# A share for every edge: one lookup list walked by POOL alone, or split between POOL's gathers and one-hot products on chip

## The reference

```
def _L2_gnn_ref(feature, src, dst, W_s, W_t, W_attn, W_fc, b_fc):
    z = proj_s[src] + proj_t[dst]
    z = jnp.where(z >= 0, z, NEG_SLOPE * z)
    e = (z @ W_attn.T)[:, 0]
    m = jax.ops.segment_max(e, src, num_segments=n)
    e_exp = jnp.exp(e - m[src])
    denom = jax.ops.segment_sum(e_exp, src, num_segments=n)
    alpha = e_exp / denom[src]
    msg = feature[src] * alpha[:, None]
    agg = jax.ops.segment_sum(msg, dst, num_segments=n)
```

## Time and profile before

| | us |
|---|---|
| median of 3 runs (9783.69 to 9792.57) | 9786.06 |
| the profiled execution, its own time | 9778.72 |
| its span in the trace | 9777.0 |
| POOL's first instruction of `share_in` | at 6859.21 |
| end of the last gather of `share_in` | at 7421.35 |
| PE's first instruction of the next phase | at 7428.20 |

### The profile page before, as it was taken

One profiled execution on the slowest core, in us unless ns is written; L12 is line 12 of the kernel. 1 busy time (PEld: TensorE's weight loads), 2 busy tenths in 40 slices (PEclk: granted clock), 3 DMA queues, 4 the chain that ended last, 5 costly groups with the idle time before them and its releaser, 6 DMA issues. The chain is left out here.

```text
span 9777.0 us, 155051 instructions
## 1 busy us (share of the span) xinstructions
PE 6076.9 (62%) x21338; PEld 3661.3 (37%) x21339; DVE 5653.9 (58%) x19482; ACT 3099.9 (32%) x10799; POOL 4876.5 (50%) x5997
## 2 busy tenths in 40 slices
PE   4666877756768887677999945444003678500277
PEld 3554233324543433455666611111002557400165
DVE  4666988873558776354445455555001458755664
ACT  2665022211554443254444400000000466411046
POOL 1333177756632212664444467775666652455252
PEclk8998577777989998799999966666556999755599
DMA  2332000004876654596666632332002797411057
GB/s 84 134 132 96 0 1 1 1 1 151 284 256 215 214 206 173 181 302 233 236 234 234 222 98 90 91 90 66 1 0 76 234 302 217 144 42 42 23 178 229
DMA packets 779248, 1347.62 MB, mean 138 GB/s; under 512 B 139839, under 2 KB 546391, under 8 KB 779156
## 3 DMA queue, kind: packets, MB, share of 16 engines
q1 hardware_dynamic: 208564, 650.10, 19.0%
q10 hardware_dynamic: 413792, 410.91, 13.2%
q0 software_dynamic: 156800, 285.65, 10.5%
HBM read 751.95 MB, written 594.32 MB: 138 GB/s over the span
## 5 line engine op out<-in xcount | busy, mean ns | idle before, releaser
L1435 PE MATMUL node_p_out<-w,node_h_t 128*128 128x512 f32 (+3 forms) x7840 | 2614.7, 466 | 379.1 <-ACT node_h_t L1463 141.9
L990 PE MATMUL merge_banks<-merge_rows,merge_mask 128*128 x6264 | 1680.7, 425 | 744.0 <-SPq L959 464.5
L1435 PEld LDWEIGHTS node_p_out<-w,node_h_t 128*128 128x128 f32 x7840 | 1357.1, 197 | 1077.7 <-issue 734.9
L990 PEld LDWEIGHTS merge_banks<-merge_rows,merge_mask 128*128 128x128 f32 x6264 | 1278.1, 211 | 1146.6 <-issue 954.0
L972 DVE TENSOR_SCALAR merge_mask<-ramp,dst_at,soft_at_step 128x128 f32<-128x128 f32 x2349 | 847.2, 366 | 1069.8 <-PE merge_banks L990 950.3
L1078 POOL DMA_INDIRECT merge_rows<-h,merge_take_i x1176 | 1125.1, 957 | 655.6 <-issue 249.4
L1022 ACT COPY merge_total<-merge_banks 128x256 f32<-128x256 f32 x1568 | 577.6, 369 | 1251.5 <-PE merge_banks L990 1135.4
L1613 PE MATMUL score_table<-score_at_high,score_at_low 128*128 128x392 f32 x784 | 565.6, 827 | 588.8 <-DVE score_at_high L1574 584.0
L1009 ACT COPY merge_banks<-merge_held 128x256 f32<-128x256 f32 x1568 | 588.1, 376 | 897.5 <-DMA merge_held<-own 643.3
L1353 POOL TENSOR_TENSOR node_inv_std<-node_var,node_minus_half 128x4 f32<-128x4 f32 x392 | 437.0, 1115 | 751.0 <-DVE node_var L1311 750.0
L1463 ACT ACTIVATE node_h_t<-node_p_turn 128x256 f32<-128x256 f32 x1568 | 594.7, 385 | 349.6 <-PE node_p_turn L1413 344.9
(11 more groups left out here) (409 smaller groups left out, 9678.3 us busy)
## 6 DMA issues: line engine op xcount, KB each, us to landing
h<-node_out SPq DMA_DIRECT2D x196, 512.0 KB, 5.7
merge_held<-own ACTq DMA_DIRECT2D x196, 512.0 KB, 5.8
x<-merge_total ACTq DMA_DIRECT2D x196, 512.0 KB
node_x<-x SPq DMA_DIRECT2D x196, 512.0 KB, 5.9
node_x<-in_x SPq DMA_DIRECT2D x194, 512.0 KB
h<-node_rows_h SPq DMA_DIRECT2D x98, 512.0 KB, 2.7
merge_held<-h ACTq DMA_DIRECT2D x98, 512.0 KB
mix<-merge_total ACTq DMA_DIRECT2D x98, 512.0 KB
```

What stands on the lines that cost most here:

```text
L990: nc.tensor.matmul(banks[:, bass.ds(nc.s_assert_within(at[2 * j + 1], 0, (BANKS - 1) * 512, skip_runtime_bounds_check_because=small), D)], ...
L1435: ins = nc.tensor.matmul(p_out[w][g % banks][:, 0:n], h_t[g][:, c * P:(c + 1) * P], matrix[:, c, :], start=c == 0, stop=c == 1)
```

## The change

Of the 49 groups of eight tiles, the first `GATHERED` = 25 (200 tiles) are still gathered by POOL, and the last `TURNED` = 24 (192 tiles) are looked up on chip by the other engines, in the same phase.

- In `src_out`, PE transposes the four blocks of `share` into PSUM, and DVE copies them to `table`, which is the tile `by_place`. The four DMAs to `shares` stay.
- In `share_in`, POOL copies eight columns of places at once, issues eight gathers, and itself copies a group's eight results into `out` (`keep`). The copy of group i-1 stands behind the gathers of group i. POOL waits for its own copies. DVE has no part in it any more.
- DVE splits all places into `high` and `low` with four chained instructions. For each of its 192 tiles it makes `at_low` and `at_high` (`hots`), and three tiles later it picks (`pick`): the `tensor_tensor_reduce` over 392 columns of `at_high` and the product in PSUM. Each eight tiles it copies the picked columns to `out`.
- PE transposes `at_low` of tile t (`turn`), then multiplies the table by `low_t` of tile t-1 (`look_up`), f32 with 392 columns.
- ACT copies the transposed `at_low` from PSUM to the f32 `low_t`.
- These four streams share rings of RING = 4 buffers, with waits on each other's counts.

```
-def shares_by_edge(nc, k, shares, out):
+def shares_by_edge(nc, k, shares, table, out):
...
+    NI, HALF, RING = k.NT // U, U // 2, 4
+    TURNED = NI // 2
+    GATHERED = NI - TURNED
+    START = GATHERED * U
...
+            def gathers(i, half, uses):
+                nc.gpsimd.tensor_copy(take_i[:, half, :], columns(k.pos_i, i * U, U)).then_inc(indexed, 1)
+                pool.wait_ge(indexed, i + 1)
+                pool.sem_inc(turn_pool, 1)
                 for j in range(U):
...
+                    nc.gpsimd.indirect_dma_start(got[:, half, j:j + 1], None, shares,
+                                                 bass.IndirectOffsetOnAxis(take_i[:, half, j:j + 1], 0)).then_inc(got_in[half], 16)
+
+            def keep(i, half, uses):
+                pool.wait_ge(got_in[half], 16 * U * uses)
+                pool.sem_inc(turn_pool, 1)
+                nc.gpsimd.tensor_copy(columns(out, i * U, U), got[:, half, :]).then_inc(copied, 1)
+                pool.wait_ge(copied, i + 1)
+                pool.sem_inc(turn_pool, 1)
+
+            gathers(0, 0, 1)
+            gathers(1, 1, 1)
+            keep(0, 0, 1)
+            with pool.Fori(1, GATHERED // 2) as i:
+                gathers(2 * i, 0, i + 1)
+                keep(2 * i - 1, 1, i)
+                gathers(2 * i + 1, 1, i + 1)
+                keep(2 * i, 0, i + 1)
+            if GATHERED % 2:
+                gathers(GATHERED - 1, 0, GATHERED // 2 + 1)
+            keep(2 * (GATHERED // 2) - 1, 1, GATHERED // 2)
+            if GATHERED % 2:
+                keep(GATHERED - 1, 0, GATHERED // 2 + 1)
...
+            chain = Chain(dve, digits)
+            chain(nc.vector.tensor_scalar(part_i[:], k.pos_i[:], 7, None, ALU.logical_shift_right))
+            chain(nc.vector.tensor_copy(high[:], part_i[:]))
+            chain(nc.vector.tensor_scalar(part_i[:], k.pos_i[:], P - 1, None, ALU.bitwise_and))
+            chain(nc.vector.tensor_copy(low[:], part_i[:]))
+
+            def hots(t, j):
+                later(dve, turned, t - RING + 1)
+                nc.vector.tensor_scalar(at_low[j % RING][:], k.ramp[:, 0:P], columns(low, t + START), None, ALU.is_equal
+                                        ).then_inc(low_hot, 1)
+                later(dve, picked_n, t - RING + 1)
+                nc.vector.tensor_scalar(at_high[j % RING][:], k.ramp[:, 0:k.NT], columns(high, t + START), None, ALU.is_equal
+                                        ).then_inc(high_hot, 1)
+
+            def pick(t, j):
+                dve.wait_ge(rowed, t + 1)
+                dve.wait_ge(high_hot, t + 1)
+                later(dve, picked_n, t)
+                nc.vector.tensor_tensor_reduce(junk[:], at_high[j % RING][:], p_row[j % RING][:, 0:k.NT], 1.0, 0.0,
+                                               ALU.mult, ALU.add, picked[:, j:j + 1]).then_inc(picked_n, 1)
+                if j == U - 1:
+                    dve.wait_ge(picked_n, t + 1)
+                    nc.vector.tensor_copy(columns(out, t + START - U + 1, U), picked[:]).then_inc(kept, 1)
+                    dve.wait_ge(kept, t // U + 1 if isinstance(t, int) else (t >> 3) + 1)
+
+            walk(dve, [(0, hots), (3, pick)])
...
+            def turn(t, j):
+                pe.wait_ge(low_hot, t + 1)
+                later(pe, low_copied, t - 1)
+                nc.tensor.transpose(p_turn[j % 2][:, 0:P], at_low[j % RING][:], k.ident_bf[:]).then_inc(turned, 1)
+
+            def look_up(t, j):
+                pe.wait_ge(low_copied, t + 1)
+                later(pe, picked_n, t - RING + 1)
+                nc.tensor.matmul(p_row[j % RING][:, 0:k.NT], low_t[j % RING][:], table[:, 0:k.NT], start=True, stop=True
+                                 ).then_inc(rowed, 1)
+
+            walk(pe, [(0, turn), (1, look_up)])
...
+                act.wait_ge(turned, t + 1)
+                later(act, rowed, t - RING + 1)
+                nc.scalar.copy(low_t[j % RING][:], p_turn[j % 2][:, 0:P]).then_inc(low_copied, 1)
...
-def shares_by_source(nc, k, cols, shares):
+def shares_by_source(nc, k, cols, shares, table):
...
+            dve.wait_ge(turned, 1)
+            nc.vector.tensor_copy(table[:], p[:]).then_inc(s_done, 1)
+
+        @block.tensor
+        def _(pe):
+            pe.wait_ge(step, 2)
+            for b in range(B):
+                ins = nc.tensor.transpose(p[:, b * P:(b + 1) * P], share[:, b, :], k.ident[:])
+            ins.then_inc(turned, 1)
```

More of the change, by code:

```diff
@@ L1100, in merge, with walk, tile, later @@
     ph.close()
-def shares_by_edge(nc, k, shares, out):
+def shares_by_edge(nc, k, shares, table, out):
     ph = Phase(nc, "share_in")
[L1107 to L1111, removed]
+    NI, HALF, RING = k.NT // U, U // 2, 4
+    TURNED = NI // 2
+    GATHERED = NI - TURNED
+    START = GATHERED * U
+    take_i, got = ph.sb("take_i", [P, 2, U], I32), ph.sb("got", [P, 2, U])
+    part_i = ph.sb("part_i", [P, k.TC], I32)
+    high, low = ph.sb("high", [P, k.TC]), ph.sb("low", [P, k.TC])
+    at_low = [ph.sb(f"at_low{n}", [P, P], BF16) for n in range(RING)]
+    at_high = [ph.sb(f"at_high{n}", [P, k.NT], BF16) for n in range(RING)]
+    low_t = [ph.sb(f"low_t{n}", [P, P]) for n in range(RING)]
+    junk = ph.sb("junk", [P, k.NT], BF16)
+    p_turn = [ph.ps(f"turn{n}", [P, 1024], BF16) for n in range(2)]
+    p_row = [ph.ps(f"row{n}", [P, 512]) for n in range(RING)]
+    picked = ph.sb("picked", [P, U])
+    indexed, copied, turn_pool, digits, low_hot, high_hot, turned, low_copied, rowed, picked_n, kept = (ph.sem(n) for n in (
+        "indexed", "copied", "turn_pool", "digits", "low_hot", "high_hot", "turned", "low_copied", "rowed", "picked", "kept"))
+    got_in = ph.sem_per_slot("got_in", 2)
+    def walk(engine, stages):
+        deepest = max(lag for lag, _ in stages)
+        def tile(i, j):
+            for lag, stage in stages:
+                t = i * U + j - lag
+                if isinstance(t, int) and not 0 <= t < TURNED * U:
+                    continue
+                stage(t, (j - lag) % U)
+        for j in range(U):
+            tile(0, j)
+        with engine.Fori(1, TURNED) as i:
+            for j in range(U):
+                tile(i, j)
+        for j in range(deepest):
+            tile(TURNED, j)
+    def later(engine, sem, count):
+        if not isinstance(count, int) or count > 0:
+            engine.wait_ge(sem, count)
     with nc.Block() as block:
@@ L1114, in _ @@
         def _(pool):
-            def tiles(i, first):
+            def gathers(i, half, uses):
+                nc.gpsimd.tensor_copy(take_i[:, half, :], columns(k.pos_i, i * U, U)).then_inc(indexed, 1)
+                pool.wait_ge(indexed, i + 1)
+                pool.sem_inc(turn_pool, 1)
                 for j in range(U):
[L1117 to L1126, removed]
@@ L1127, in _ @@
-            peeled(pool, NI, tiles)
+                    nc.gpsimd.indirect_dma_start(got[:, half, j:j + 1], None, shares,
[6 more added lines that the diff above has]
+                pool.sem_inc(turn_pool, 1)
@@ L1137, in shares_by_edge, with _, copies @@
+        @block.scalar
+        def _(act):
+            def copies(t, j):
+                act.wait_ge(turned, t + 1)
+                later(act, rowed, t - RING + 1)
+                nc.scalar.copy(low_t[j % RING][:], p_turn[j % 2][:, 0:P]).then_inc(low_copied, 1)
+            walk(act, [(0, copies)])
     ph.close()
@@ L1749, in shares_by_source @@
     ph = Phase(nc, "src_out")
-    step, stored = ph.sem("step"), ph.sem("stored")
+    step, stored, turned, s_done = (ph.sem(n) for n in ("step", "stored", "turned", "done"))
+    p = ph.ps("p", [P, k.TC])
     with nc.Block() as block:
@@ L2040, in gnn_kernel @@
         score_sources(nc, k, from_src, to_dst, by_place)
-        shares_by_source(nc, k, by_place, shares)
-        shares_by_edge(nc, k, shares, share)
+        shares_by_source(nc, k, by_place, shares, by_place)
+        shares_by_edge(nc, k, shares, by_place, share)
         to_rows(nc, k, "rows2", share, rows)
```

## The result

The changed kernel takes 9522.47 us (median of 4 runs, 9516.57 to 9529.82) against 9784.88 for the kernel before (median of 4 runs, 9775.10 to 9792.57). The ratio is 0.9733, with a 95% interval of 0.9716 to 0.9750. The prediction was 9513 us, with a range of 9499 to 9552.

What follows compares the result with a forecast made beforehand. The prediction took POOL's chain of issue, 1.43 us a tile, as the bound. 288.6 - 562.1 + 0.5 (tail) + 0 (table) = -273 us, from 9786.06 to 9513 us, with a range of 9499 to 9552 for 8 in 10.

Steps and rivals of the forecast that it cites:

- POOL's beat as the bound: In `share_in`, POOL's chain of issue sets the time: 288.6 us to its last gather's end, against 562.1 before.
- the loop ends: POOL's 11 loop ends in `share_in`, now behind a drained wait, at 0.30 us each: 3.3 us (bounds 0 and 6.2).
- DVE's delay: DVE working beside POOL in `share_in` lengthens each gather by 0.01 us: 2 us (bounds 0 and 16).
- The first landing wait: `keep`'s wait for gathers issued a group (10.7 us) before is covered, against 2.1 us of landing; uncovered, 2 us each.
- The lookup's pace: DVE takes 1.30 us a tile for 192 tiles in `share_in`, 249 us; the lookup side ends after 255 us.
- the upper bound of 1.69: DVE's us a tile if alternating instructions don't overlap, adding records of `at_low`, `at_high`, a pick and 0.10: 324 us.
- Rival 2: DVE holds POOL's gathers up in `share_in`, by 82 us (9595) or 162 us (9675); chance 0.10.
- The tail: After the last gather: 2.1 us landing as before, then POOL's copy and wait replace DVE's copy: +0.5 us.
- The table: Transposes and copy to the table in `src_out` lie beside 3.7 us of stores: 0 us, bound 2.
- likeliest case: POOL ends last in `share_in`, the lookup side before it: 9500 to 9523 us, chance 0.62.
- Rival 3: The lookup in `share_in` runs in series, 3.33 us a tile, 639 us, so the kernel is slower: 9866 us; chance 0.02.
- Rival 1: The lookup side binds `share_in`, by PE's low clock or DVE's added records, 295 to 327 us: 9519 to 9551; chance 0.23.

Runs made afterwards that it cites:

- x1: Changed kernel without DVE's, PE's and ACT's programs in `share_in`, so POOL's 200 gathers run alone: 9500.33 us.
- x2: Changed kernel without POOL's program in `share_in`, so only the 192 tiles looked up on chip: 9427.53 us.
- x4: Changed kernel with the lags of `pick` and `look_up` 0 in place of 3 and 1, each tile's lookup in series: 9844.53 us.
- x10: Changed kernel with TURNED = 27 in place of 24 (216 tiles looked up, 176 gathered), the same kernel as x5: 9475.10 us, ratio 0.9689.
- x9: The changed kernel again, unedited, as control: 9512.66 us against 9773.21 for the kernel before, ratio 0.9723.
- x5: Changed kernel with TURNED = 27, on another chip where the kernel before took 10353.14 us: 10190.84 us, ratio 0.9847.
- x8: Changed kernel with all 392 tiles looked up and no POOL program, on the other chip (kernel before 10353.14 us): 10227.99 us.
- x7: Changed kernel with the last group's copy into `out` on DVE instead of POOL, on the other chip (kernel before 10353.14 us): 10185.09 us.
- x3: Changed kernel with TURNED = 0: POOL gathers all 49 groups in its new order, no lookup on chip: 9774.78 us.
- x12: x6's kernel (`at_low` on ACT, TURNED = 30) with the deeper rings of x11: 9440.12 us, ratio 0.9651.
- x11: x10 with eight ring buffers, four PSUM buffers for transposes, `pick` six tiles behind and `look_up` three: 9471.12 us, ratio 0.9688.
- x6: Changed kernel with `at_low` made by two ACT instructions and TURNED = 30, on the other chip (kernel before 10353.14 us): 10190.70 us, ratio 0.9847.

## Why the prediction was right

- **POOL's beat as the bound.** Right. 267.2 + 16.1 + 3.3 + 2 = 288.6 us were forecast, and it is 285.4. Of the difference, `keep` is the term that was sized too high. x1 has 282.1 - 267.2 = 14.9 us beyond the gathers' own beat, in place of 19.4: 23 `keep`s of 0.46 are 10.6 (forecast 16.1), the loop ends add 2.4 (forecast 3.3), and the other 1.9 are POOL's pause at the 113th gather, a term that the prediction didn't have. Its rows of before held it: the beat gave 557.6 us where the trace had 562.1, and two pauses are 3.5 of the 4.5 between. DVE's delay was sized too low, 3.3 in place of 2. The first landing wait was covered, as forecast.
- **The lookup's pace.** 1.30 us a tile was forecast, 1.19 measured. The picks and hots overlap across kinds as they do within one: x2 has 1.09, and the sum of records that gave the upper bound of 1.69 plays no part. The pick was sized too high: it was taken as 0.60 from start to the next instruction, and is 0.49. The clock was forecast as a mean between its levels, and is 1.00 in all windows but the first. POOL's 1.44 us for each of the 192 tiles doesn't follow from the prediction's sum, which gives 288.6 / 192 = 1.50; nothing else hangs on it.
- **POOL and DVE on one another.** The median of a gather went from 944 (x1) to 947 ns, `at_high` from 424 (x2) to 462. The forecast that DVE is the one that pays held. Rival 2, by which POOL waits for every one-hot, would have had gathers of 1.4 to 1.8 us; the longest is 1.15. The Trainium skill ("SBUF — State Buffer", section "Who interferes with whom") states a full block of the one that comes second. The traces agree that both kinds get longer at times, by up to 0.21 and 0.23 us, and x1 puts the whole cost for POOL at 3.3 us, where rival 2 had 82 or 162.
- **The tail.** Forecast +0.5 us, measured 9.8 - 6.9 = 2.9 more. This step failed in its mechanism: it took what follows the last gather as landing, copy and barrier. It is POOL's drain, and it was so before the change too: there it ended 6.1 us behind the last gather, with landing and DVE's copy beside it. Now it takes 7.24 us and begins 1.8 us behind the last gather, after POOL's own wait and copy. x4 and x10, where POOL is through before the lookup, have 1.2 us from the last pick to the next phase.
- **The table.** Hidden, as forecast: 3.76 us of stores against 3.72.
- **The total.** The phase fell by 273.7 us where 273 were forecast, in part because its errors cancel (3.2 too much on POOL, 2.4 too little in the tail), and that is luck. The medians fell by 262.4 and, in x9, 260.6, against 273.7 and 274.0 for the phase. Of the 11 to 13 us between, no cause is shown. They put the result at the upper edge of the likeliest case, 9522.47 for 9500 to 9523. The start of the phase, behind unchanged code, lies between 6853.6 (x4) and 6880.2 (changed) in the profiled executions of the changed kernel and its variants outside x5 to x8, and at 6859.2 in the one of before, so a single pair of traces can't place them.
- **Rival 3.** Its price was right (3.35 for 3.33), in part by luck: in x4's rows the product takes 1.71 us to the pick in place of 1.51, the other steps are 1.47 in place of 1.82, and the end of a group of eight, which the price had left out, adds 1.1 us (7203.36 to 7207.68 from pick to pick, for 3.2 inside a group). x4 shows how near it lies: two lags are all that separates it. **Rival 1** came true under the condition of x5 and x7, by late starts and not by the clock or DVE's records, which is a mechanism that the prediction didn't have.

## What to carry to other kernels

When one engine's issue chain bounds a phase and others idle, a second way on the idle engines pays beside it, and the split is found by dividing: tiles by pace on either side, plus each side's fixed end. Here neither way alone comes near: all on POOL the phase takes 563.9 us (x3), all looked up 436 (x8, on the other chip), split 233.0 (x12). Count each side's end too: an engine that has to drain shouldn't be the last. 24 groups of 49 left 50 us of slack, 27 closed it, and every gain in the lookup's pace moves the point further (30 groups at 0.94 us). Give such a pipeline some depth between its engines: without any it was a loss (x4), and twice the depth together with `at_low` on ACT is what made the last version work.

## What the runs showed of the hardware that was not expected

- POOL's drain at the end of a phase in which it gathered is long and repeats to the nanosecond: 7239 ns behind 200 gathers (changed, x1, x4, x7, x9), 5279 behind 176 (x5, x10, x11), 3319 behind 152 (x6, x12), 4626 behind 392 (x3), and 34 without any (x2, x8). It goes with the gathers since POOL's last pause, 87, 63, 39 and 55: 134 ns and 81.67 ns for each give all four to the nanosecond. The kernel before, with 67 since its last pause, has 9563 ns from a start that lies ahead of its last gathers, so it can't be set against this. What pause and drain do is not shown, and a split chosen to have few gathers behind a pause wasn't tried. The drain is free where another engine ends later.
- PE's granted clock was 1.00 from 7420 to 7820 in x8, with its matmuls 88% to 91% busy in each 20 us, and 0.50 from 6860 to 7500 in x4, with 56% to 61% in each 40 us.
- Under the condition of x5 to x8 the kernel before ran 5.8% longer (10353 for 9785 us). 452 of these 568 us lie in `rank_src`'s second pass, by x6's trace. There, as in the changed phase, DVE, PE and ACT hand over to each other while POOL gathers. `score_sources`, in which POOL gathers too, isn't longer: the copy of `score_table` comes 1154 us behind the memset of `soft_by_place` in x6, 1159 in the changed kernel. The gain of 3% of a split of 27 shrank to 1.5% there.
